# Feed-forward stage: normalised rows on ACT, inner rounding on POOL, input side one tile ahead in place of two

## The reference

```python
# x: (64, 64, 256), ctx: (64, 256, 256)
x = x + xattn(layernorm(x), ctx, ctx)      # 16 heads, stage 1
x = x + attn(layernorm(x))                 # causal, 16 heads, stage 2
x = x + ffn(layernorm(x))                  # stage 3, the one that changes

def act_quant(x):                          # per row
    scale = 127.0 / clip(max(abs(x), axis=-1), 1e-05)
    return clip(round(x * scale), -128, 127) / scale

def bitlinear(x, w): return act_quant(x) @ weight_quant(w).T    # weights in {-1, 0, 1} / scale

def ffn(x):                                # 256 -> 1024 -> 256
    return bitlinear(silu(bitlinear(x, w_gate)) * bitlinear(x, w_up), w_down)
```

## Time and profile before

| | |
|---|---|
| median of 3 runs | 971.3 us (970.1 to 972.48) |
| profiled execution | 967.37 us |
| its span, first to last instruction | 965.2 us |
| PE busy | 906.7 us (94%) |
| DVE busy | 793.8 us (82%) |
| ACT busy | 689.4 us (71%) |
| POOL busy | 320.2 us (33%) |
| mean granted TensorE clock | 0.995 |

### The profile page before, as it was taken

The page is one execution under the profiler, slowest core; times in us unless marked ns, Lnnn a source line. Parts: engine busy times, 40 slices in busy tenths (PEclk is TensorE's granted clock), DMA queues, the critical chain, the costliest instruction groups (busy, mean ns, idle before and its releaser), DMA issues. The chain is left out here.

```text
span 965.2 us, 29774 instructions
## 1 busy us (share of the span) xinstructions
PE 906.7 (94%) x9778; PEld 731.1 (76%) x9794; DVE 793.8 (82%) x1711; ACT 689.4 (71%) x2012; POOL 320.2 (33%) x452
## 2 busy tenths in 40 slices
PE   5999999999999999999999979999999996999997
PEld 4888888888888888888888857777777773555554
DVE  3877888888888888888788748888888886999997
ACT  3677876767777676776767747676676675888897
POOL 1323222232222322332232235545545541222221
PEclk9999999999999999999999999999999998999999
DMA  8111111111111111111111000000000000000001
GB/s 299 46 38 33 38 38 44 40 33 38 38 44 38 36 38 41 38 38 43 38 33 38 11 1 3 0 0 0 0 0 0 0 1 1 28 27 28 28 28 39
DMA packets 31602, 31.47 MB, mean 33 GB/s; under 512 B 3280, under 2 KB 30800, under 8 KB 31568
## 3 DMA queue, kind: packets, MB, share of 16 engines
q1 hardware_dynamic: 30720, 30.73, 10.4%
q10 hardware_dynamic: 848, 0.33, 0.1%
HBM read 26.86 MB, written 4.19 MB: 32 GB/s over the span
## 5 line engine op out<-in xcount | busy, mean ns | idle before, releaser
L474 ACT ACTIVATE probs<-psum,nmax 128x256 f32<-128x256 f32 x512 | 237.3, 487 | 93.5 <-DVE nmax L434 93.5
L434 DVE TENSOR_REDUCE nmax<-psum 128x2 f32<-128x512 f32 x256 | 159.1, 684 | 30.0 <-PE psum L305 30.0
L318 PE MATMUL psum<-id_sb,probs 128*128 128x128 f32 x1024 | 137.4, 278 | 13.9 <-ACT probs L474 13.8
L318 PEld LDWEIGHTS psum<-id_sb,probs 128*128 128x128 f32 x1024 | 113.1, 142 | 29.4 <-ACT probs L474 27.8
L482 POOL TENSOR_TENSOR rstd<-vare,minus_half 128x1 f32<-128x1 f32 x96 | 52.7, 549 | 234.1 <-DVE vare L372 231.6
L491 POOL TENSOR_TENSOR cl<-c_sb,ch 128x512 fp32r<-128x512 f32 x64 | 81.5, 1274 | 99.7 <-ACT ch L449 99.7
L474 ACT ACTIVATION_READ_ACCUMULATOR probs<-psum,nmax 128x1 f32 x512 | 112.7, 220 | 0.0
L455 ACT ACTIVATE probsT<-psum 128x512 f32<-128x512 f32 x160 | 90.9, 619 | 10.0 <-PE psum L318 10.0
L498 POOL TENSOR_TENSOR rm<-rinv,hm_sb 128x256 f32<-128x256 f32 x64 | 39.7, 620 | 132.5 <-DVE rinv L411 132.5
L305 PE MATMUL psum<-k_sb,qb 32*128 32x256 f32 x1024 | 77.4, 400 | 0.0
L939 PE MATMUL psum<-wb_all,xqT 128*128 128x512 bf16 x240 | 65.8, 386 | 10.6 <-DVE probs L839 7.3
(11 more groups left out here) (113 smaller groups left out, 2166.4 us busy)
## 6 DMA issues: line engine op xcount, KB each, us to landing
c_sb<-in_ctx_t SPq DMA_DIRECT2D x64, 256.0 KB, 2.7
x_sb<-in_x SPq DMA_DIRECT2D x32, 128.0 KB, 2.1
out<-y_sb SPq DMA_DIRECT2D x32, 128.0 KB, 1.7
w_all<-in_w_gate SPq DMA_DIRECT2D x1, 1024.0 KB, 7.4
w_all<-in_w_up SPq DMA_DIRECT2D x1, 1024.0 KB, 9.3
w_all<-in_w_down SPq DMA_DIRECT2D x1, 1024.0 KB, 11.5
wqkv_sb<-in_w_qkv SPq DMA_DIRECT2D x1, 768.0 KB, 6.5
wq_sb<-in_wq ACTq DMA_DIRECT2D x1, 256.0 KB, 4.1
```

The costliest lines, as they stand in the source:

```text
L318: last = nc.tensor.transpose(sp[g][:, c:c + P], probs[:, 2 * g + u, kh * P:(kh + 1) * P], id_sb[:])
L434: nc.vector.tensor_reduce(nmax[:, 2 * g:2 * g + 2], sp[g].rearrange("p (u s) -> p u s", u=2), AX.X, ALU.max, negate=True).then_inc(max_don ...
L474: nc.scalar.activation(probs[:, j, :], sp[g][:, u * S:(u + 1) * S], ACT.Exp, bias=nmax[:, j:j + 1], accum_out=rsum[:, j:j + 1]).then_inc(e ...
```

## The change

`act_scale_h` is gone: the rounding of hq is issued on POOL, in `pool_fd_h`, behind fd, which now waits for hscale too. `dve_xn` leaves this stage: POOL computes nmean = -mean and nmr = -mean * rstd (`pool_shift3`), and `act_xn3` makes xn = x * rstd + nmr on ACT. The orders of all four engines are new, with the input side one tile ahead on PE and ACT and two on DVE, and DVE starts the block with the mean of tile 2 alone. The loops of ACT and POOL are unrolled. In the diff, definitions of semaphores and small buffers and the removed loop ends are cut.

```diff
+        def pool_shift3(p, t):
+            p.wait_ge(xn3_done, t)
+            p.wait_ge(stats3, t * 3 + 2)
+            nc.gpsimd.tensor_tensor(nmean[:], mv[:, 0:1], minus_one[:], ALU.mult)\
+              .then_inc(nmean_done, 1)
+            pool_rstd3(p, t)
+            p.wait_ge(nmean_done, t - 1)
+            p.wait_ge(rstd3_done, t + 1)
+            nc.gpsimd.tensor_tensor(nmr[:], nmean[:], rstd[:], ALU.mult).then_inc(nmr_done, 1)
+        def act_xn3(a, t):
+            a.wait_ge(nmr_done, t - 1)
+            a.wait_ge(aq, t * 3 - 2)
+            a.wait_ge(xs_done, t)
+            nc.scalar.activation(xn[:], at(t), ACT.Identity, bias=nmr[:, 0:1],
+                                 scale=rstd[:, 0:1]).then_inc(xn3_done, 1)
...
-        def pool_fd(p, t, par):
-            p.wait_ge(hqs, t * 3 + 2)
+        def pool_fd_h(p, t, par):
+            p.wait_ge(hqs, t * 3 + 3)
             if not isinstance(t, int) or t > 1:
                 p.wait_ge(fin_done, t - 1)
+                p.wait_ge(ht_mm, t * 2 - 2)
             nc.gpsimd.tensor_tensor(fd[par][:], hmaxc[:], w_mean[:, 2:3],
                                     ALU.mult).then_inc(fd_done, 1)
+            nc.gpsimd.tensor_scalar(hq[par][:], hid[par], hscale[:, 0:1], ROUND, ALU.mult,
+                                    ALU.add).then_inc(hs_done, 1)
...
                 a.wait_ge(gate_mm, t * 2 + n + 1)
                 nc.scalar.activation(hid[par][:, half], g_ps[n], ACT.Silu,
                                      scale=fgu[par][:, 0:1]).then_inc(silu_done, 1)
-        def act_scale_h(a, t, par):
-            a.wait_ge(hqs, t * 3 + 3)
-            if not isinstance(t, int) or t > 1:
-                a.wait_ge(ht_mm, t * 2 - 2)
-            nc.scalar.activation(hq[par][:], hid[par], ACT.Copy, bias=ROUND,
-                                 scale=hscale[:, 0:1]).then_inc(hs_done, 1)
...
             def _(pe):
                 pe.wait_ge(wq_step, 36)
                 pe_gate_up(pe, 0)
-                pe_xq(pe, 1)
-                pe_gate_up(pe, 1)
-                def body(t, par, ahead2=True):
-                    if ahead2:
-                        pe_xq(pe, t + 2)
+                def body(t, par, ahead1=True):
+                    if ahead1:
+                        pe_xq(pe, t + 1)
                     if not isinstance(t, int) or t > 0:
                         pe_down(pe, t - 1)
-                    if ahead2:
-                        pe_gate_up(pe, t + 2)
+                    if ahead1:
+                        pe_gate_up(pe, t + 1)
                     pe_ht(pe, t, par)
                 body(0, 0)
...
                 with pe.Fori(1, NT // 2 - 1) as n:
                     body(n * 2, 0)
                     body(n * 2 + 1, 1)
-                body(NT - 2, 0, ahead2=False)
-                body(NT - 1, 1, ahead2=False)
+                body(NT - 2, 0)
+                body(NT - 1, 1, ahead1=False)
                 pe_down(pe, NT - 1)
             @block.vector
             def _(v):
                 v.wait_ge(y2_ev, NT)
-                dve_quant_x(v, 2)
+                dve_mean(v, LN3, 2, at(2))
                 dve_hid(v, 0, 0)
-                def body(t, par, ahead3=True, ahead1=True):
+                def body(t, par):
                     dve_hmax(v, t, par)
-                    if ahead3:
-                        dve_mean(v, LN3, t + 3, at(t + 3))
                     dve_unit_h(v, t)
                     dve_scale_h(v, t)
-                    if ahead1:
+                    if t + 2 < NT:
+                        dve_absmax_x(v, t + 2)
+                        dve_scale_x(v, t + 2)
+                    if t > 0:
+                        dve_fin(v, t - 1, 1 - par)
+                    if t + 3 < NT:
+                        dve_mean(v, LN3, t + 3, at(t + 3))
+                    if t + 1 < NT:
                         dve_hid(v, t + 1, 1 - par)
-                    if ahead3:
-                        dve_xn(v, LN3, t + 3, at(t + 3), xs_done)
-                        dve_absmax_x(v, t + 3)
-                    if not isinstance(t, int) or t > 0:
-                        dve_fin(v, t - 1, 1 - par)
-                    if ahead3:
-                        dve_scale_x(v, t + 3)
-                body(0, 0)
-                body(1, 1)
-                for t in range(2, NT - 4):
+                for t in range(NT):
                     body(t, t % 2)
-                body(NT - 4, 0)
-                body(NT - 3, 1, ahead3=False)
-                body(NT - 2, 0, ahead3=False)
-                body(NT - 1, 1, ahead3=False, ahead1=False)
                 dve_fin(v, NT - 1, 1)
             @block.scalar
             def _(a):
                 act_silu(a, 0, 0)
-                act_xqt(a, 1)
-                act_silu(a, 1, 1)
-                def body(t, par, ahead2=True):
-                    if ahead2:
+                def body(t, par):
+                    if t > 0:
+                        act_ht(a, t - 1)
+                    if t + 1 < NT:
+                        act_xqt(a, t + 1)
+                    if t + 2 < NT:
+                        act_xn3(a, t + 2)
+                    if t + 1 < NT:
+                        act_silu(a, t + 1, 1 - par)
+                    if t + 2 < NT:
                         act_scale_x(a, t + 2)
-                    if not isinstance(t, int) or t > 0:
-                        act_ht(a, t - 1)
-                    if ahead2:
-                        act_xqt(a, t + 2)
-                    act_scale_h(a, t, par)
-                    if ahead2:
-                        act_silu(a, t + 2, par)
-                body(0, 0)
-                body(1, 1)
-                with a.Fori(1, NT // 2 - 1) as n:
-                    body(n * 2, 0)
-                    body(n * 2 + 1, 1)
-                body(NT - 2, 0, ahead2=False)
-                body(NT - 1, 1, ahead2=False)
+                for t in range(NT):
+                    body(t, t % 2)
                 act_ht(a, NT - 1)
             @block.gpsimd
             def _(p):
-                pool_rstd3(p, 2)
-                def body(t, par, ahead3=True, ahead2=True):
-                    if ahead2:
+                pool_shift3(p, 2)
+                def body(t, par):
+                    pool_fd_h(p, t, par)
+                    if t + 2 < NT:
                         pool_fgu(p, t + 2, par)
-                    if ahead3:
-                        pool_rstd3(p, t + 3)
-                    pool_fd(p, t, par)
-                body(0, 0)
-                body(1, 1)
-                with p.Fori(1, NT // 2 - 2) as n:
-                    body(n * 2, 0)
-                    body(n * 2 + 1, 1)
-                body(NT - 4, 0)
-                body(NT - 3, 1, ahead3=False)
-                body(NT - 2, 0, ahead3=False, ahead2=False)
-                body(NT - 1, 1, ahead3=False, ahead2=False)
+                    if t + 3 < NT:
+                        pool_shift3(p, t + 3)
+                for t in range(NT):
+                    body(t, t % 2)
```

More of the change, by code:

```diff
@@ L71, in block_kernel @@
         eps_col = sb("eps_col", [P, 1])
+        minus_one = sb("minus_one", [P, 1])
+        nmean = sb("nmean", [P, 1])
+        nmr = sb("nmr", [P, 1])
         wq_sb = sb("wq_sb", [P, KT, D])
@@ L789, in block_kernel @@
         xn3_done = sem("xn3_done")
+        nmean_done = sem("nmean_done")
+        nmr_done = sem("nmr_done")
         aq = sem("aq")
@@ L1050, in _ @@
                 nc.vector.memset(eps_col[:], EPS).then_inc(const_set, 1)
+                nc.vector.memset(minus_one[:], -1.0).then_inc(const_set, 1)
                 dve_stats(v, LN1, 0, x_sb[:], (x_in, 16))
```

## The result

The changed kernel takes 973.73 us (median of 17 runs, 970.73 to 975.86), the kernel before 971.38 us (17 runs, 968.84 to 974.1). The ratio is 1.0022, with a 95% interval of 1.0012 to 1.0032: about 2 us slower, where 0.5 us faster was forecast. It lies within the 0.3% that I called "no change", but on the other side of it.

What follows compares the result with a forecast made beforehand. DVE's pace was taken as the bound in the feed-forward. DVE gains 2.5 us, the start takes 0.8 and the end about 1.2: 0.5 us faster, 970.8 us against 971.3, range 966 to 979.

Steps and rivals of the forecast that it cites:

- three gaps: On DVE, instructions placed directly behind what they read (hid-hmax, hmax-hmaxc, amax-amaxc) cost 0.12 more each, 0.36 us a tile.
- H: Time of the 128x1024 rounding on POOL, taken as 1.2 us, with 1.0 to 2.36 as the range.
- ring: hscale(t) through POOL rounding, transposes, hqT, gate and up to hid(t+2) and its hscale: H + 7.67 for two tiles, 4.44 each.
- The start: Start of the feed-forward: tile 2's input work mostly falls between hid(0) and hid(1), so hid(1) comes 0.83 us later.
- The change on DVE: DVE's period per tile: xn leaves, minus 0.44, gaps add 0.36; 4.58 us in place of 4.66.
- The step from hid(1) to hid(29): 28 periods of 4.58 minus 0.39 put hid(29) at 946.12 against 947.80, 1.7 us gained there.
- The end: Last tiles: the ring decides, about 1.2 us lost; rounding's end to last y_sb 2.56 as before, at 961.96 against 962.45.
- The unrolled loops: ACT's and POOL's loops becoming unrolled code: put at nothing, with a bound of 1 us.
- A: Rival: POOL rounding priced by what it writes, 1.6 to 2.36, so the ring sets the pace; 978 at 1.89; chance 0.17.
- B: Rival: the ring is longer than summed at H = 1.2; 0.6 more makes the period 4.74, 975 us; chance 0.17.
- C: Rival: the three gaps of 0.12 don't appear on DVE; the ring sets the pace at 4.32, 962 us; chance 0.12.
- D: Rival: POOL and DVE block each other, amaxc waiting until hq ends, 1.1 us a tile; 1004 us; chance 0.04.

## Why the prediction was wrong

Its mechanism held for the period: DVE's pace, three gaps that return most of xn's 0.44 us, H near 1.2, a ring close below. The sign failed on terms of the sum, and at the end on PE's durations, taken at the full clock. In the stretch from hid(0) to the last y_sb it had minus 0.5 us, measured plus 1.69:

- **The start** (0.83 later at hid(1)): right. hid(0) to hid(1) is 4.19 in place of 3.36.
- **The change on DVE** (4.58): the period is 4.61. Each gap came as taken from the earlier trace rows; 0.03 lies in the small spacings (amaxc to y_sb 0.30, where amaxc to hmax had been 0.26; bn_stats to hid 0.64 for 0.61). Times 28: 0.9 us.
- **The step from hid(1) to hid(29)** ("minus 0.39, no y_sb in the first"): wrong. That interval lies in the body of tile 1, which has y_sb(0); it measured 4.62. And one interval of each kernel is 0.36 too long (5.01 before, the twelfth; 4.97 after, the thirteenth); the 947.80 that I compared with held it, my sum did not. 0.75 us together. Its cause stays open: the profile names no engine that DVE waited for there.
- **The end** ("from its end to the last y_sb 2.56 as before"): wrong by 0.84. The sum had PE waiting 2 us for hq(31) and kept its durations at the full clock. H was 0.08 lower, twice, and hscale(29) to hid(31) without it 0.15 shorter (5.73 in all), for silu and not the up matmuls ended last: with the handoffs 0.34 back.

0.9 + 0.75 + 0.84 - 0.34 = 2.15, of the 2.18 us missed. The step that failed most is thus the size of what was gained by hid(29): 1.7 us forecast, measured 0.0 (from hid(1) to hid(29) 129.53 us in place of 130.36, and the start took the same 0.83). The unrolled loops were put at nothing; in the stretch the sum leaves 0.03 us for them.

The rivals: A and B didn't occur (H 1.12, ring under DVE's period; the doubled rounding shows what A would have been). The ring itself was drawn through gate and up alone; the one through xn and amax, which the prediction had as "cost nothing", is the first to bind when H grows. In the change xn was ready about 0.5 us before amax (890.85 and 891.32) and the silu about 0.55 us before hid, so neither cost anything there. C is refuted. D is refuted as I wrote it, since amaxc took 0.15 at 891.75 in the middle of hq; but its mechanism exists, for xn of 256 elements, and I had not weighed what removing xn from DVE was good for. In the chances it made no difference, because the change has both moves. The Trainium skill's port-bound 1.03 cycles an element (GPSIMD Engine Reference, "Elementwise — side-by-side cycle accounting") gave an estimate of 1.1 us for the rounding, and the trace agrees with 1.12; by its 1.8 cycles the estimate was 1.7, with which the trace disagrees.

The difference in the runs (2.35 us in the medians, 1.2 to 3.1 by the interval) has these 1.69 us within it; whether the remainder is more clock lost elsewhere stays open.

## What to carry to other kernels

Price an instruction by the spacing that it has in its new place, not by its duration: behind its own producer each costs some 0.12 us more here, and an order that puts three such pairs together gave back nearly the whole worth of a removed instruction. When work is moved to POOL, look which DVE instruction would then run beside it. Follow every instruction that waits on the moved work, not only the longest path: here amax, behind xn, bound before hid did. And count a stretch against the trace from the first to the last instruction, its odd intervals included, before comparing a sum with it; where PE will idle near an end, take its durations at the lower clock.

## What the runs showed of the hardware

- A DVE tensor_scalar of 128x256 in fp32 between SBUF tiles waits for a running POOL instruction to end (0.88 for 0.40 us). Lying beside POOL's rounding, others keep their time: the reduction amax 0.42, bn_stats 0.42, y_sb 0.48 and hid 1.28, which read PSUM, and the one-element amaxc 0.15.
- POOL's tensor_scalar with a scale per partition takes 1.12 us for 1024 elements a partition, as fast as ACT (1.15).
- An idle time of 2.1 us on PE, at the end of the block, was followed by a granted clock of half (0.50): down product 1.87 in place of 1.03; eight unused matmuls in the gap kept it up. It fell only after PE had begun again: with the rounding doubled, behind 2.83 us of idle time, the transposes ran at 1.00 and the down product after them at 0.53. And without any edit the same kernel's hid(0) moved by 3.7 us with the clock.
